# A gated cross-attention kernel: the two gates ride in W's first transfer, and tanh runs later on ScalarE

## What is computed

```python
def xattn(h, v):                                   # h: normalised x, v: context
    p = softmax(einsum('bsd,bvd->bsv', h, v))
    return einsum('bsv,bvd->bsd', p, v)

def ffn(h, W, b, lora_down, lora_up, down_aux, up_aux):
    low = up_aux @ (lora_up @ (lora_down @ down_aux))
    return h @ W.T + b + h @ low.T

x = x + tanh(g_xattn[0]) * xattn(layernorm(x), context)
x = x + tanh(g_ffn[0])   * ffn(layernorm(x), ...)
```

## Time and profile before

| | |
|---|---|
| Time, median of 3 runs | 313.3 us (312.91 to 313.48) |
| The profiled execution | 313.07 us |
| Its span, first to last instruction | 311.3 us |
| PE busy | 302.0 us (97%) |
| DVE, ACT, POOL busy | 235.0 us (75%), 187.5 us (60%), 226.5 us (73%) |
| The chain that ended last | PE 94%, DMA 2%, DVE 1%, ACT 1% |

### The profile page before, as it was taken

How to read it: one execution, slowest core, us unless ns; L and a number is a source line. 1 busy time by engine, 2 the same in 40 slices (tenths; PEclk the granted TensorE clock), 3 DMA queues, 4 the chain that set the end, 5 groups by cost and what they waited for, 6 DMA issues and landing times.

```text
span 311.3 us, 6483 instructions
## 1 busy us (share of the span) xinstructions
PE 302.0 (97%) x2086; PEld 286.1 (92%) x2086; DVE 235.0 (75%) x743; ACT 187.5 (60%) x546; POOL 226.5 (73%) x276
## 2 busy tenths in 40 slices
PE   5999999999999999999999999999999999999992
PEld 3779999998999999999899999999899999999992
DVE  2887778895787887798497778888588777777765
ACT  3665656664576656666466566656466656566552
POOL 3747887788487777877577877778478778877763
PEclk9999999999999999999999999999999999999998
DMA  5845455345594455555294565544197554444013
GB/s 162 305 147 225 151 187 175 149 174 205 182 272 175 166 187 177 204 202 205 73 266 192 202 226 202 204 171 162 76 274 254 203 201 150 169 179 170 27 59 135
DMA packets 16614, 56.39 MB, mean 181 GB/s; under 512 B 2129, under 2 KB 2129, under 8 KB 16580
## 3 DMA queue, kind: packets, MB, share of 16 engines
q1 hardware_dynamic: 15856, 54.64, 50.5%
q10 hardware_dynamic: 724, 1.32, 1.3%
HBM read 35.84 MB, written 16.78 MB: 169 GB/s over the span
## 4 chain that ended last, share of the span: by engine, by line
PE 94%; DMA 2%; DVE 1%; ACT 1%; issue 0%; POOLq 0%; ACTq 0%; POOL 0%; DVEq 0%
PE y_ps L555 66%; PE y_ps L586 10%; PE a_ps L581 10%; PE c_ps L531 3%; PE y_ps L563 2%; DMA c_rows<-in_ctx 2%; PE y_ps L626 1%; PE y_ps L631 1%; PE a_ps L543 1%; PE c_ps L522 1%; PE y_ps L647 0%; PE a_ps L547 0%; PE y_ps L508 0%; DVE o_sb L753 0%; DVE v_lo L818 0%
## 5 line engine op out<-in xcount | busy, mean ns | idle before, releaser
L555 PE MATMUL y_ps<-wc,xT 128*128 128x334 f32 (+1 forms) x1536 | 228.2, 302 | 0.0
L555 PEld LDWEIGHTS y_ps<-wc,xT 128*128 128x128 f32 x1536 | 214.4, 189 | 2.1
L334 POOL TENSOR_TENSOR x_bias<-x,bias_g 128x512 f32<-128x512 f32 x63 | 81.4, 1292 | 63.1 <-DVE x L715 63.1
L322 POOL TENSOR_TENSOR xT<-xt_raw,xT 128x512 fp32r<-128x512 f32 x64 | 83.1, 1298 | 0.1
L423 ACT ACTIVATE expd<-y_ps,neg_max,rs 128x77 f32<-128x77 f32 x64 | 26.6, 416 | 80.2 <-DVE neg_max L705 80.2
L437 ACT ACTIVATE squares<-x,x_nmean 128x512 f32<-128x512 f32 x64 | 46.4, 725 | 16.4 <-DVE x_nmean L723 16.4
L350 POOL TENSOR_TENSOR rs<-stat_eps,half_neg 128x2 f32<-128x2 f32 (+1 forms) x67 | 46.0, 687 | 5.2
L753 DVE SCALAR_TENSOR_TENSOR o_sb<-y_ps,rs,x_bias 128x512 f32<-128x512 f32 x64 | 48.0, 750 | 1.4 <-issue 0.8
L586 PEld LDWEIGHTS y_ps<-stacks,pT 109*128 109x128 f32 (+1 forms) x256 | 39.8, 191 | 5.4
L715 DVE SCALAR_TENSOR_TENSOR x<-a_ps,x_sb 128x512 f32<-128x512 f32 x64 | 43.6, 682 | 0.2 <-PE a_ps L581 0.2
L694 DVE BATCH_NORM_STATS2 bn<-x_sb 128x6 f32<-128x512 f32 x64 | 43.8, 684 | 0.0
(11 more groups left out here) (80 smaller groups left out, 193.7 us busy)
## 6 DMA issues: line engine op xcount, KB each, us to landing
x_sb<-in_x SPq DMA_DIRECT2D x32, 512.0 KB, 4.2
xt_raw<-in_xt SPq DMA_DIRECT2D x31, 512.0 KB, 5.1
out<-o_sb SPq DMA_DIRECT2D x31, 512.0 KB, 3.0
stacks<-v_hi SPq DMA_DIRECT2D x3, 308.0 KB
stacks<-v_hi SPq DMA_DIRECT2D x3, 256.0 KB
stacks<-v_lo SPq DMA_DIRECT2D x3, 256.0 KB
w_rows<-in_w SPq DMA_DIRECT2D x2, 256.0 KB, 6.1
w_rows<-in_w ACTq DMA_DIRECT2D x2, 256.0 KB, 6.8
```

Of the source, the lines that this page charges most:

```text
L322: pool.tensor_tensor(xT[:, k % TRING, 1, :, :], xt_raw[:, k % XRING // UNIT, k % UNIT, :, :], xT[:, k % TRING, 0, :, :].bitcast(F32), ALU. ...
L334: pool.tensor_tensor(x1_bias[:, q, :], x1[:, j, :], bias_g[:, :], ALU.add).then_inc(x1b_ready, 1)
L555: mm = pe.matmul(y_half(k, h)[:, 0:n], xT[:, k % TRING, part, c, :], wc[:, c, w, h * H:h * H + n], start=(c == 0 and part == 0 and w == 0) ...
```

## The change

The gates are written by the host as two extra columns in front of W's block 0, so that they land with `ld_w[0]`. For that W is laid out on the host as 128 rows, each with 2 + 4 x 512 numbers: a row holds the two gates and then row p of each of the four blocks. Block 0's transfer takes 514 numbers of each row, the other three 512; in `w_all` on the chip every block now starts 8 bytes further than it did. The transfer of the gates is gone. On ScalarE tanh and `ctx_rows_hi(0)` stand behind the mean of W's block 1 and ahead of `up_st`.

```diff
-        b_row = sb("b_row", [P, D + 2])
+        b_row = sb("b_row", [P, D])
...
-        w_rows = sb("w_rows", [P, KC, D])
+        w_all = sb("w_all", [P, 2 + KC * D])
+        w_rows = w_all[:, 2:2 + KC * D].rearrange("p (c d) -> p c d", c=KC)
...
         def load_w(eng, c):
-            eng.dma_start(w_rows[:, c, :], W[c * P:(c + 1) * P, :]).then_inc(ld_w[c], 16)
+            at, end = 2 + c * D if c else 0, 2 + (c + 1) * D
+            eng.dma_start(w_all[:, at:end], W[:, at:end]).then_inc(ld_w[c], 16)
...
         def _(act):
-            act.dma_start(b_row[:, D:D + 2], b_gates[D:D + 2].partition_broadcast(P)).then_inc(ld_gates, 16)
             act.dma_start(c_rows[:, :], ctx_in[0]).then_inc(ld_ctx, 16)
...
-            act.wait_ge(ld_gates, 16)
-            act.activation(tg[:, :], b_row[:, D:D + 2], ACT.Tanh).then_inc(tg_ok, 1)
-            ctx_rows_hi(0)
-
             act.wait_ge(low_mm, 1)
...
             prep(0, TURN)
             w_mean(1, 0)
+            act.wait_ge(ld_w[0], 16)
+            act.activation(tg[:, :], w_all[:, 0:2], ACT.Tanh).then_inc(tg_ok, 1)
+            ctx_rows_hi(0)
             act.wait_ge(low_mm, 2)
             act.activation(up_st[:, :], up_bank(), ACT.Copy).then_inc(up_hi_ok, 1)
             w_mean(2, 1)
...
+    gates = np.broadcast_to(np.concatenate([g_xattn, g_ffn]), (128, 2))
+    rows = np.reshape(np.transpose(np.reshape(L0_ffn_W, (d // 128, 128, d)), (1, 0, 2)), (128, d * d // 128))
...
-        "x": x, "xt": xt, "ctx": ctx_1024, "w": L0_ffn_W,
-        "b_gates": np.concatenate([L0_ffn_b, g_xattn, g_ffn]),
+        "x": x, "xt": xt, "ctx": ctx_1024, "w": np.concatenate([gates, rows], axis=1),
+        "b": L0_ffn_b,
```

More of the change, by code:

```diff
@@ L18, with build_kernel @@
 YRING = 3
-def build_kernel(nc, x, xt_in, ctx_in, W, b_gates, low_in, low_out, out):
+def build_kernel(nc, x, xt_in, ctx_in, W, b, low_in, low_out, out):
     B, S, D = x.shape
@@ L146, in build_kernel @@
         ld_w = [sem(f"ld_w{i}") for i in range(KC)]
-        ld_b, ld_gates, ld_in, ld_out, ld_ctx = (sem(n) for n in ("ld_b", "ld_gates", "ld_in", "ld_out", "ld_ctx"))
+        ld_b, ld_in, ld_out, ld_ctx = (sem(n) for n in ("ld_b", "ld_in", "ld_out", "ld_ctx"))
         zeroed, ident_ok, tg_ok, biasg_ok = (sem(n) for n in ("zeroed", "ident_ok", "tg_ok", "biasg_ok"))
@@ L266, in _ @@
             load_x(0, 0)
-            sp.dma_start(b_row[:, 0:D], b_gates[0:D].partition_broadcast(P)).then_inc(ld_b, 16)
+            sp.dma_start(b_row[:, 0:D], b.partition_broadcast(P)).then_inc(ld_b, 16)
             sp.wait_ge(zeroed, 1)
```

## The result

| | before | after |
|---|---|---|
| Time, median (22 executions each) | 313.36 us (312.24 to 314.62) | 311.88 us (311.21 to 314.41) |
| Ratio to before | | 0.996 (0.9945 to 0.9975) |
| Span of the profiled execution | 311.3 us | 309.6 us |

The change made the kernel faster: by 1.5 us by the medians, and by 0.4% or 1.25 us by the ratio, which also feels the two executions at 314.4. A second set gave 312.09 against 312.99, a ratio of 0.9981 (0.9958 to 1.0003), so a gain that by itself isn't clear of no change. My 312.8 had half a microsecond of gain; the measured median of 311.88 is even 0.2 under the low end of my range, and close to the rival "the gain is larger" (312.2).

What follows compares the result with a forecast made beforehand. TensorE was taken to bound the kernel, with only its setup able to move: 0.48 + 0.15 = 0.63 ahead, times 0.75 for the clock, 0.47; 313.3 - 0.47 = 312.8 against the median, range 312.1 to 313.6.

Steps and rivals of the forecast that it cites:

- the gain is larger: Rival, chance 0.35: without tiny packets `low_in_sb` lands up to 0.65 sooner, clock's rise comes along; 0.48 + 0.65 = 1.13, 312.2.
- my own signs of being wrong: Context lands at 6 or later, TensorE waits for block 1, 2 or 3, or clock's rise moves more than work ahead.
- What bounds: TensorE is busy 97% of the span; only its setup up to `first_product` at 18.60 moves, the loop follows rigidly.
- The gates' transfer, removed: Head of ScalarE's queue: context sooner, L522 gains 0.48; L513 gains 0.15 from `low_in_sb`; TensorE 0.63 ahead.
- both my bounds of 5.4 and 5.8: Context's landing: 5.80 with its own 5.08 kept, 5.4 if it takes the time of the gates' transfer.
- Its reason: The larger-gain rival's ground: the gates' tiny packets gone, `low_in_sb` on the other queue lands up to 0.65 sooner.
- tanh and v_hi, moved: ScalarE before `up_st`: their 0.92 fills the 0.86 idle; L492's margin before the fifth transpose shrinks from 0.55 to 0.07.
- The rival that ScalarE eats the gain: Chance 0.12: block 1 lands 0.6 later, at 9.1, delaying `up_st` and L492; at 1 us nearly all 0.48 gone, 313.3.
- W's layout: W's transfers, blocks 8 bytes further: put at 0, since misaligned `low_out` rows show no surcharge.
- The estimate of 0.3: W's block 3: by the misalignment rule, 32 packets to an engine add some 0.3 us, absorbed by 0.7 of room.
- The clock: TensorE's rise from 1.2 to 2.4 GHz: keeps 0.63 if it comes along, 0.31 if it stays; taken 0.63 x 0.75 = 0.47.

Runs made afterwards that it cites:

- tanh early: Changed kernel with tanh and `v_hi` back ahead of `squares`, waiting for W's block 0: 311.70 against 312.99 (ratio 0.9955), again 312.02 against 313.30 (0.9964).
- `v_lo` early: Changed kernel with tanh, `v_hi` ahead of `squares` and `ctx_rows_lo` directly behind VectorE's block 0: 311.50 against 313.30 (0.9955), again 311.95 against 312.85 (0.9967).

## Why the prediction was right, and where it was not

The direction, the place and most of the steps held; sizes did not. The first median is 0.2 outside my range, and two of my own signs of being wrong came: TensorE waited for block 2, and the clock's rise moved by more than the work ahead of it.

- **What bounds.** Right: only the setup moved, and what follows `first_product` was 292.7 in both kernels.
- **The gates' transfer, removed.** Right that this is the part that counts: the other two alone gave 1.0001 and 1.0002, and the landing of the context and of what follows moved with it in every profile. (Moved to third place instead of removed it gave 0.9987, which is not clear of 1.) The term was mis-sized. I had 0.48 + 0.15 = 0.63 for TensorE's head and it measured 1.15. `low_in_sb` came 0.38 sooner in this pair of profiles where I took 0.15 out of 0 to 0.65, and the 0.27 from L522 following L513 at once was missing altogether: I had moved L522 with its length of 0.78. It takes 0.77 to 0.78 in every profile in which TensorE had waited for it and 0.51 wherever it follows at once at 1.2 GHz. The rival's 1.13 agrees with the 1.15 by luck, as its terms were 0.48 and 0.65. The context landed at 4.5, sooner than both my bounds of 5.4 and 5.8, which brought nothing more, as L513 decides.
- **Its reason.** I put the rival's larger gain on the tiny packets. For the context that is mostly wrong, as one piece costs 1.7 where 128 cost 2.0; for `low_in_sb` it stays open, since it landed by 4.73 even with the pieces at the head, in the layout's run.
- **tanh and v_hi, moved.** Right as a mechanism, with a margin that I gave as 0.07: the cover was gone by 0.23, because TensorE was 1.15 ahead and ScalarE only 0.4. The rival that ScalarE eats the gain came true to this part, though through L513 and not through block 1.
- **W's layout.** Right at 0: ratio 1.0001 with all of W 8 bytes off. The rule of the Trainium skill, "DMA: Bandwidth & Descriptors", section "How a descriptor splits into AXI transactions", on one more transaction for a misaligned piece was no reason to fear it here. The estimate of 0.3 that I had worked out by it is not contradicted either: W landed 0.2 to 0.3 later in that one profile, and the kernel had the room.
- **The clock.** This step failed. I let the rise either stay or come along with the work, 0.31 to 0.63 of a gain, and took three quarters. In the first pair of profiles it came 3.3 us sooner for 1.15 of head start, which gave 0.82 on top. In the second profile of the changed kernel it came 3.0 later than before: the clock's rise is not a factor on the gain but a quantity of its own. In profiles of the same program it came at 11.5 and 17.9 (the changed kernel), 11.3 and 14.3 (tanh early), 11.6 and 13.3 (`v_lo` early), and `first_product` ended 2.6, 0.9 and 0.9 later for it. It also depends on TensorE's work ahead: 0.85 less of filler made the kernel 1.5 to 2.2 slower. What decides it in a single execution stays open. The first profile was therefore a lucky pair with 1.74; the medians say 1.5 and 0.9, the ratios 1.25 and 0.6.

## What to carry to other kernels

The first transfer on a queue should be the one that the chain waits for; one of 1 KB ahead of it cost 1.7 to 2.0 us, in one piece or in 128. Where TensorE starts at 1.2 GHz, filler in a place where it would wait anyway cost nothing here, and taking 0.85 us of it out cost 1.5 to 2.2; in the profile of that run the clock's rise came last of all, at 18.7. For changes of this size compare the medians of some 20 executions, in more than one set, not two profiles, and look for a second group among them.

## What the runs showed of the hardware

The profile's granted clock says full speed from the start of the span, while products take twice their later time until the rise; in the setup its rows show the slow level only after a later fall, as in the run with more filler (0.56). Until the rise, durations are the better witness. By the products' lengths and the changes that the traces record, the rise came between 11.3 and 18.7 us in thirteen of the fourteen profiles, whose TensorE streams differ by little, and at 5.7 in the run with one more filler.

VectorE's `v_lo`, with two inputs in SBUF, took 1.23 in the kernel before, 1.72 in the changed one and 0.74 where GpSimd was idle. The first two lines are the kernel before, the others the changed one.

```profile
12.08 1.27 POOL L322 TENSOR_TENSOR xT<-xt_raw,xT 128x512 fp32r<-128x512 f32 x1
12.67 1.23 DVE L661 SCALAR_TENSOR_TENSOR v_lo<-c_rows,tg,v_hi 77x512 fp32r<-77x512 f32 x1
...
11.63 1.28 POOL L324 TENSOR_TENSOR xT<-xt_raw,xT 128x512 fp32r<-128x512 f32 x1
11.74 1.72 DVE L661 SCALAR_TENSOR_TENSOR v_lo<-c_rows,tg,v_hi 77x512 fp32r<-77x512 f32 x1
```

In both, `v_lo` ends 0.55 after GpSimd's instruction (13.90 - 13.35 and 13.46 - 12.91), wherever it started, as if its work began only then. By the Trainium skill, "SBUF — State Buffer", section "Who interferes with whom", a VectorE instruction with two inputs in SBUF contends with a GpSimd instruction that reads SBUF; the durations agree.
